# SSM output projection as three products of halves, normalisation on ScalarE, halves split on VectorE and GpSimd, x reloaded after the stage

## The reference, cut to what matters

```python
proj = x @ Wi                                  # 256 -> 512 (xs) + 64 (B) + 64 (C)
xc = silu(causal_conv(xs, cw, 4 taps) + cb)    # depthwise over the tokens
h = A * h + u_t * b_t ; y = h . c_t            # scan over 128 tokens, A = -0.5
x = layer_norm(y @ Wo + x) * g + b             # Wo: 512 -> 256
```

## Time and profile before

| | value |
|---|---|
| median of 3 runs | 1272.3 us (1270.44 to 1274.01) |
| profiled execution | 1271.9 us, span 1270.2 us |
| mean granted TensorE clock | 0.955 |
| TensorE busy, whole span | 1136.6 us (89%) |
| VectorE, ScalarE, GpSimd busy | 835.3 us (66%), 650.7 (51%), 663.3 (52%) |
| output projection L303 | 640 passes, 143.5 us |
| DMA | 53.73 MB, 42 GB/s on average |

### The profile page before, as it was taken

How to read it: one execution, slowest core, us unless ns; L and a number is a source line. 1 busy time by engine, 2 the same in 40 slices (tenths; PEclk the granted TensorE clock), 3 DMA queues, 4 the chain that set the end, 5 groups by cost and what they waited for, 6 DMA issues and landing times.

```text
span 1270.2 us, 21225 instructions
## 1 busy us (share of the span) xinstructions
PE 1136.6 (89%) x6835; PEld 886.8 (70%) x6835; DVE 835.3 (66%) x1882; ACT 650.7 (51%) x1905; POOL 663.3 (52%) x705
## 2 busy tenths in 40 slices
PE   3999999999996999999997699984699999986984
PEld 3788888888885788888876477763366666655862
DVE  6788988889883666666676578875433333324795
ACT  2555555555542655555555388882122444224873
POOL 3175766757653224334254577661357556642664
PEclk9999999999997999999999799996799999997995
DMA  4001001010100000000010123610523222322001
GB/s 149 20 1 58 23 17 62 17 62 0 34 2 0 1 2 1 1 1 1 1 51 18 59 76 126 250 43 33 143 43 49 44 43 43 50 34 67 1 26 42
DMA packets 38206, 53.73 MB, mean 42 GB/s; under 512 B 8448, under 2 KB 33024, under 8 KB 36576
## 3 DMA queue, kind: packets, MB, share of 16 engines
q1 hardware_dynamic: 29376, 42.28, 10.0%
q0 software_dynamic: 8736, 10.25, 5.1%
HBM read 40.78 MB, written 11.74 MB: 41 GB/s over the span
## 4 chain that ended last, share of the span: by engine, by line
PE 43%; ACT 7%; issue 7%; DVE 7%; POOL 3%; DMA 1%; POOLq 0%; ACTq 0%; DVEq 0%
PE bank L1515 11%; PE bank L1532 5%; ACT x_prob L1182 5%; PE bank L44 4%; PE bank L46 3%; PE bank L45 3%; PE bank L643 2%; PE bank L671 2%; PE bank L654 1%; PE bank L1272 1%; PE bank L1524 1%; PE bank L2001 1%; PE bank L1285 1%; POOL a_prob L810 1%; PE bank L1213 1%
## 5 line engine op out<-in xcount | busy, mean ns | idle before, releaser
L414 DVE SCALAR_TENSOR_TENSOR ssm_conv<-bank,conv_w,ssm_conv 128x508 f32<-128x508 f32 (+2 forms) x240 | 159.2, 729 | 10.1 <-ACT ssm_conv L350 10.1
L704 ACT ACTIVATE a_prob<-a_prob,a_neg_max 128x128 f32<-128x128 f32 x256 | 99.7, 391 | 117.8 <-DVE a_neg_max L750 117.8
L1515 PE MATMUL bank<-expert_raw,x_kept_next_t 128*128 x312 | 148.5, 599 | 1.2 <-ACT x_kept_next_t L1594 1.2
L303 PE MATMUL bank<-w_out,ssm_u 128*128 128x256 f32 x640 | 143.5, 382 | 0.0
L810 POOL TENSOR_TENSOR a_prob<-a_prob,a_inv 128x512 f32<-128x512 f32 x64 | 66.7, 1042 | 136.3 <-DVE a_inv L755 136.3
L303 PEld LDWEIGHTS bank<-w_out,ssm_u 128*128 128x128 f32 x640 | 119.9, 190 | 17.9
L508 POOL TENSOR_TENSOR act_t_lo<-ssm_turned,act_t_hi 128x512 fp32r<-128x512 f32 x40 | 51.6, 1290 | 97.5 <-ACT ssm_turned L375 97.5
L1459 POOL DMA_INDIRECT x_rows<-e_y,e_index x39 | 62.9, 1612 | 75.2 <-ACT e_y L1622 71.6
L1738 DVE COPY e_h_t<-bank 128x512 f32<-128x512 f32 x39 | 27.0, 692 | 105.3 <-PE bank L1524 102.0
L1182 ACT ACTIVATE x_prob<-bank,x_neg_max 128x128 f32<-128x128 f32 x256 | 89.9, 403 | 11.5 <-DVE x_neg_max L1159 11.5
L1069 POOL TENSOR_TENSOR x_prob<-x_prob,x_inv 128x512 f32<-128x512 f32 x64 | 67.1, 1054 | 42.1 <-DVE x_inv L1163 41.6
(11 more groups left out here) (328 smaller groups left out, 3010.2 us busy)
## 6 DMA issues: line engine op xcount, KB each, us to landing
expert_raw<-in_experts_laid SPq DMA_DIRECT2D x8, 1536.0 KB, 8.2
attn_raw<-in_attn_w_laid SPq DMA_DIRECT2D x4, 1024.0 KB, 7.6
w_in_raw<-in_L_attn_in_proj_w SPq DMA_DIRECT2D x5, 640.0 KB, 8.4
w_out<-in_L_attn_out_proj_w SPq DMA_DIRECT2D x5, 512.0 KB, 3.9
x_res<-in_x SPq DMA_DIRECT2D x4, 512.0 KB, 5.6
x_context<-in_ctx_t_laid SPq DMA_DIRECT2D x8, 256.0 KB, 3.8
z_rows<-x_kept_next_z SPq DMA_DIRECT2D x8, 256.0 KB, 2.1
x_rows<-x_res SPq DMA_DIRECT2D x8, 256.0 KB, 2.4
```

The costliest lines, as they stand in the source:

```text
L303: mm = pe.matmul(UWY[h][:, s * D:(s + 1) * D], u[:, g % 2, c, t:t + P], w_out[:, c, :], start=(c == 0), stop=(c == KI - 1))
L414: op = dve.scalar_tensor_tensor(out=acc, in0=xs, scalar=conv_w[:, c, TAPS - 1 - back:TAPS - back], in1=acc, op0=ALU.mult, op1=ALU.add)
L704: e = act.activation(prob[:, m % 4, i, :], prob[:, m % 4, i, :], ACT.Exp, bias=neg_max[:, m % 4, i:i + 1], accum_out=total[:, m % 4, i:i + 1])
L1515: mm = pe.matmul(bank[:, :], rows_t[:, t % 2, k, :], W[:, bass.ds(at + (column + k * FFN), FFN)], start=(k == 0), stop=(k == KD - 1))
```

## The change

- The output projection becomes `product`: w_out and u are each held as a high and a low half in fp32r. ScalarE writes silu(conv) twice, as `u_hi` and whole, in place, into `conv`; GpSimd subtracts (`split_u`) into `u_lo`. ScalarE makes w_out's high half, VectorE its low half, once a layer.
- The low half of the turned rows is taken by VectorE straight from the bank; `ssm_turned` and its copy go.
- The normalisation goes from VectorE to ScalarE, as res x rstd + shift with shift = -mean x rstd made by GpSimd for all four sequences of a group at once. It is done in the group after, between taps 1 and 2 of the next group. `finish` (ln_g, ln_b) moves with it.
- w_in is split in two parts, in group 2 of a layer.
- u_hi takes the memory of x, which is loaded again when the attention stage begins; GpSimd waits for it (`attn_ln_loaded` 48) before its attention work. `attn_raw` holds all four weights (4 MB, one transfer) in the memory of their low halves.
- GpSimd's loop over layers is written out. A constant of -1 is made at the start.

Names of semaphores, the declarations of tiles, and helpers that only move are left out of the diff.

```diff
-def split_w_in(pool, mem, layer, in_use=None):
+def split_w_in(pool, mem, layer, part, in_use=None):
...
+    chunks = lambda x: x[:, :, :].rearrange("p k (c n) -> p k c n", n=P)[:, :, (slice(0, KI + 1, KI), slice(1, KI))[part], :]
+    if part == 0:
+        pool.wait_ge(names["w_in_loaded"], layer * 16 + 16)
+        if in_use is not None:
+            pool.wait_ge(in_use, layer * GROUPS * KI)
+    pool.tensor_copy(chunks(hi), chunks(raw)).then_inc(names["w_in_split"], 1)
...
-                sp.wait_ge(names["w_in_split"], layer + 1)
+                sp.wait_ge(names["w_in_split"], layer * 4 + 4)
...
-                sp.wait_ge(uw_ready, layer * (2 * GROUPS) + 2 * GROUPS)
+                sp.wait_ge(names["w_out_split"], layer * 2 + 2)
                 mem["load_w_out"](sp, layer + 1)
-                sp.wait_ge(mem["attn_w_split"], layer * GROUPS + GROUPS)
...
+            sp.dma_start(mem["attn_raw"][:, :, :], io["attn_w_laid"].rearrange("a p n -> p a n")).then_inc(mem["attn_w_loaded"], 16)
             with sp.Fori(0, LAST) as layer:
-
-                sp.dma_start(mem["attn_raw"][:, :], io["attn_w_laid"][bass.ds(layer, 1)].rearrange(
-                    "a p n -> p (a n)")).then_inc(mem["attn_w_loaded"], 16)
...
-                pe.wait_ge(names["w_in_split"], layer + 1)
+                pe.wait_ge(names["w_in_split"], layer * 4 + 2)
...
                                  k == 0, k == KD - 1)
                 mm.then_inc(bc_ready, 1)
                 for c in range(KI):
+                    if c == 1 and g == 0:
+                        pe.wait_ge(names["w_in_split"], layer * 4 + 4)
...
-                    pe.wait_ge(tr_copied, n * 2 + h)
+                    pe.wait_ge(tr_low, n * 2 + h)
...
-                pe.wait_ge(u_ready, n * KI + KI)
+                pe.wait_ge(u_split, n * KI + KI)
                 if g == 0:
-                    pe.wait_ge(names["w_out_loaded"], layer * 16 + 16)
+                    pe.wait_ge(names["w_out_split"], layer * 2 + 2)
...
                         for c in range(KI):
-                            mm = pe.matmul(UWY[h][:, s * D:(s + 1) * D], u[:, g % 2, c, t:t + P],
-                                           w_out[:, c, :], start=(c == 0), stop=(c == KI - 1))
+                            mm = product(pe, UWY[h][:, s * D:(s + 1) * D], [x[:, g % 2, c, t:t + P] for x in (u_hi, u_lo)],
+                                         [x[:, c, :] for x in w_out], c == 0, c == KI - 1)
                     mm.then_inc(uw_ready, 1)
...
-                for c in range(KI):
+
+            def taps(layer, g, chunks, first=False):
+                n = layer * GROUPS + g
+                for c in chunks:
                     act.wait_ge(xs_ready, n * KI + c + 1)
                     if not (first and g == 0):
-                        act.wait_ge(u_ready, n * KI - KI + c + 1)
+                        act.wait_ge(u_split, n * KI - KI + c + 1)
...
-                    nc.scalar.activation(u[:, g % 2, c, :], conv[:, c, :], ACT.Silu).then_inc(u_ready, 1)
+                    act.activation(u_hi[:, g % 2, c, :], conv[:, c, :], ACT.Silu)
+                    act.activation(conv[:, c, :], conv[:, c, :], ACT.Silu).then_inc(u_ready, 1)
+
+            def split_w_out(layer):
+                act.wait_ge(names["w_out_loaded"], layer * 16 + 16)
+                act.activation(w_out[HI][:, :, :], mem["w_out_raw"][:, :, :], ACT.Copy).then_inc(names["w_out_split"], 1)
+
+            def normalise(layer, g):
+                n = layer * GROUPS + g
+                act.wait_ge(shift_ready, n + 1)
+                for h in range(2):
+                    for s in range(2):
+                        i = 2 * h + s
+                        act.activation(res[:, h, s, :], res[:, h, s, :], ACT.Identity, bias=shift[:, i:i + 1],
+                                       scale=rstd[:, i:i + 1]).then_inc(z_ready, 1)
...
-                act.activation(ACT_T[HI][:, :, t:t + 2 * P], bank, ACT.Copy)
-                if not (layer_is(layer, 0) and g == 0 and h == 0):
-                    act.wait_ge(tr_low, n * 2 + h)
-                act.activation(turned[:, :, :], bank, ACT.Copy).then_inc(tr_copied, 1)
-
+                act.activation(ACT_T[HI][:, :, t:t + 2 * P], bank, ACT.Copy).then_inc(tr_copied, 1)
+
+            split_w_out(0)
             front(0, 0, first=True)
+            taps(0, 0, range(KI), first=True)
             silu(0, 0, range(KI), first=True)
 
             def layer_steps(layer):
                 first, last = layer_is(layer, 0), layer_is(layer, LAST)
                 for g in range(GROUPS):
                     ahead = (layer, g + 1, first) if g < GROUPS - 1 else None if last else (layer + 1, 0)
+                    before = (layer, g - 1) if g > 0 else None if first else (layer - 1, GROUPS - 1)
                     if ahead:
                         front(*ahead)
+                        taps(*ahead[:2], range(0, 2), *ahead[2:])
+                    if before:
+                        normalise(*before)
                     if ahead:
+                        taps(*ahead[:2], range(2, KI), *ahead[2:])
                         silu(*ahead[:2], range(0, 2), *ahead[2:])
                     copy_uw(layer, g, 0)
                     copy_uw(layer, g, 1)
-                    before = (layer, g - 1) if g > 0 else None if first else (layer - 1, GROUPS - 1)
                     if before:
                         copy_turned(*before, 0)
+                    if g == GROUPS - 1 and not last:
+                        split_w_out(layer + 1)
                     if ahead:
                         silu(*ahead[:2], range(2, KI), *ahead[2:])
                     if before:
                         copy_turned(*before, 1)
             layers(act, layer_steps)
+            normalise(LAST, GROUPS - 1)
...
-                    dve.wait_ge(stats_ready, n * 4 + 2 * h + 2)
-                    dve.sem_inc(stats_seen, 1)
-                    for s in range(2):
-                        dve.bn_aggr(mv[:, 2 * h + s, :], stats[:, 2 * h + s, :]).then_inc(aggr_ready, 1)
-                    dve.wait_ge(aggr_ready, n * 4 + 2 * h + 2)
-                    dve.tensor_scalar(ve[:, 2 * h:2 * h + 2], mv[:, 2 * h:2 * h + 2, 1], EPS, None,
-                                      ALU.add).then_inc(var_ready, 1)
-                for h in range(2):
-                    dve.wait_ge(rstd_ready, n * 2 + h + 1)
-                    for s in range(2):
-                        i = 2 * h + s
-                        dve.tensor_scalar(res[:, h, s, :], res[:, h, s, :], mv[:, i, 0:1],
-                                          ve[:, i:i + 1], ALU.subtract, ALU.mult).then_inc(z_ready, 1)
+                if not (layer_is(layer, 0) and g == 0):
+                    dve.wait_ge(z_ready, n * 4)
+                dve.wait_ge(stats_ready, n * 5 + 4)
+                dve.sem_inc(stats_ready, 1)
+                for i in range(GS):
+                    dve.bn_aggr(mv[:, i, :], stats[:, i, :]).then_inc(aggr_ready, 1)
+                dve.wait_ge(aggr_ready, n * 4 + 4)
+                dve.tensor_scalar(rstd, mv[:, 0:GS, 1], EPS, None, ALU.add).then_inc(var_ready, 1)
+
+            def split_w_out(layer):
+                dve.wait_ge(names["w_out_split"], layer * 2 + 1)
+                dve.tensor_tensor(w_out[LO][:, :, :], mem["w_out_raw"][:, :, :], w_out[HI][:, :, :].bitcast(F32),
+                                  ALU.subtract).then_inc(names["w_out_split"], 1)
+
+            def turned_low(layer, g, h):
+                n = layer * GROUPS + g
+                t = g * GT + 2 * h * P
+                dve.wait_ge(tr_copied, n * 2 + h + 1)
+                dve.tensor_tensor(ACT_T[LO][:, :, t:t + 2 * P], TR[:, :].rearrange("p (k t) -> p k t", k=KD),
+                                  ACT_T[HI][:, :, t:t + 2 * P].bitcast(F32), ALU.subtract).then_inc(tr_low, 1)
+
...
                     decayed(layer, g)
                     if ahead:
                         convolve(*ahead, 1)
+                    before = (layer, g - 1) if g > 0 else None if first else (layer - 1, GROUPS - 1)
+                    if before:
+                        turned_low(*before, 0)
                     norm(layer, g)
+                    if before:
+                        turned_low(*before, 1)
+                    if g == GROUPS - 1 and not last:
+                        split_w_out(layer + 1)
             layers(dve, layer_steps)
+            for h in range(2):
+                turned_low(LAST, GROUPS - 1, h)
...
-            def finish(layer, g):
+            def invert(layer, g):
 
                 n = layer * GROUPS + g
-                for h in range(2):
-                    pool.wait_ge(var_ready, n * 2 + h + 1)
-                    pool.tensor_tensor(ve[:, 2 * h:2 * h + 2], ve[:, 2 * h:2 * h + 2], neghalf[:, 0:2],
-                                       ALU.pow).then_inc(rstd_ready, 1)
+                pool.wait_ge(var_ready, n + 1)
```

(82 more changed lines are left out.)

51 lines of the change are left out of this document (22 added, 29 removed).

## The result

The changed kernel takes 1249.4 us (1248.35 to 1250.04) beside 1271.8 of the kernel before (1270.44 to 1274.01): ratio 0.9825, interval 0.9811 to 0.9839, 22.4 us less. The forecast was 1254.5, range 1248 to 1267. The profiled execution took 1250.04, span 1248.2. A second measurement, with the last experiments, gave 1249.13 and 0.9823.

The account below looks back on a forecast made before the run. TensorE's queue was taken to bound the SSM stage. Gains of 18 x 1.14 = 20.5 and 0.25, less 1.0 for the end and 2.0 for lag, made 17.8 us: 1254.5 against the median, range 1248 to 1267.

Parts of the forecast that it names:

- own range: Whole kernel, if the main forecast holds without a rival: 1249.5 us with no cost, to 1260 with the larger costs.
- The bound and the product: SSM stage: TensorE's queue bounds; output projection takes 5.87 us for 7.01, saving 1.14 a group, to 16.46.
- Rival D: Output projection on TensorE: matmuls run at 109 ns, 0.53 us more gained in 20 groups, 1244 us; 3%.
- First group: Start of the SSM stage: doubled silus delay group 1's b by 1.1 us, so this group gains 0.25, not 1.14.
- The lag of GpSimd: Behind w_in's split, once a layer: late u and shift delay uw for TensorE, 0.5 us a layer, 2.0 in all.
- The end: End of the SSM stage: last u, norm, invert and ln passes run in sequence, costing 1.0 us more.
- Rival A: SSM groups: the loop of GpSimd and ScalarE becomes the bound, 7 to 14 us less gained, 1261 to 1268; 24%.
- Rival B: SSM groups: GpSimd's loop costs more than 17.60 us, so the kernel gets slower, 1279 us; 6%.
- Rival C: SSM groups: path not shortened; ScalarE's late copy delays b, low half delays turn 1; 1269 to 1276 us; 7%.
- it just fits: ScalarE's last turned copy ends 1.5 us into the next group; the next b is ready at 1.65.
- VectorE and w_out's low half: VectorE makes w_out's low half once a layer, bounds 1.4 and, waiting for a GpSimd pass, 2.7 us.
- x and attn_raw: Loads for attention: x under 14.5 us with cover 26, attn_raw 15 to 30 us; cost nothing, attn_raw 1 at worst.

Follow-up runs that it names:

- a1: The changed kernel with its output projection as 16 fp32 products again, on the high halves alone; 1273.6 us, ratio 1.0022.
- b1: The kernel before with its output projection as 48 single-pass matmuls on stand-in operands, no step moved to another engine; 1246.4 us, ratio 0.9809.
- p1: The changed kernel plus one unneeded 128x256 GpSimd subtraction in each group of layers 0 to 3; 1253.1 us, ratio 0.9861.
- p2: The changed kernel plus one unneeded 128x512 GpSimd subtraction in each group of layers 0 to 3; 1260.7 us, ratio 0.9915.
- a3: The changed kernel with the low halves of the turned rows subtracted on GpSimd again, with ScalarE's second copy; 1285.0 us, ratio 1.011.
- s2: The changed kernel plus two unneeded 128x1024 ScalarE copies per group, ahead of its last copy of turned rows; 1252.9 us, ratio 0.9855.

## Why the prediction was right, point by point

The measured 1249.4 lies within the stated range, but at the lower end of the "own range" of 1249.5 to 1260: the mechanism was right, and nearly every cost that was set against the gain was too high.

**The bound and the product.** Right. 5.79 us measured for 5.87, a group of 16.44 for 16.46; a1 and b1 show that this term alone makes the gain. 18 groups gave 19.53 + 1.21 = 20.7 where the sum had 20.5. The pitch is 0.118, with 0.11 more in the first step. Rival D took 109 ns. The Trainium skill's page "TensorE: Matmul & The Clock Gate", section "Back-to-back issue gap", has these 109 ns (262 cycles) for 256 columns as the gap of an isolated matmul, and says that in a stream of weight loads and matmuls both set the spacing. The 118 here, weight loads included, lie above the isolated gap, in line with the second; D used the first where it doesn't hold.

**First group.** Mis-sized: 1.41 saved (0.35 + 1.06), where the sum had 0.25. The step that failed is "the last two silus still begin at 41.8, which moves group 1's b by 1.1". ScalarE's timeline of the changed kernel:

```profile
41.05 0.63 ACT L365 ACTIVATE ssm_u_hi<-ssm_conv 128x512 fp32r<-128x512 f32 x1 [0.42 <-DVE ssm_conv L440]
...
43.15 0.58 ACT L345 ACTIVATE ssm_b_t<-bank 64x512 f32<-64x512 f32 x1
```

The taps are done 0.73 earlier, at 41.05, and b is copied at 43.15 where it was at 42.97, 0.18 later and not 1.1. The first product starts at 45.54, earlier than the 45.92 of the earlier trace rows, not at 46.5. Nor does the 0.25 follow from the forecast's own numbers: 46.5 for 45.92 would leave 1.14 - 0.58 = 0.56.

**The lag of GpSimd.** The mechanism was right, its price was 0 and not 2.0. The timelines of GpSimd and ScalarE behind a split of w_in, in the changed kernel:

```profile
224.60 0.19 POOL L517 TENSOR_TENSOR ve<-mv,neg_one 128x4 f32<-128x4 f32 x1
224.76 1.01 POOL L518 TENSOR_TENSOR ve<-ve,neghalf 128x4 f32<-128x4 f32 x1
...
226.08 2.08 ACT L378 ACTIVATE ssm_res<-ssm_res,ve 128x256 f32<-128x256 f32 x4 [2.89 <-POOL ve L520]
228.07 1.43 ACT L356 ACTIVATE ssm_conv<-bank,conv_b,conv_w 128x512 f32<-128x512 f32 x2
229.39 0.62 ACT L365 ACTIVATE ssm_u_hi<-ssm_conv 128x512 fp32r<-128x512 f32 x1
229.91 0.62 ACT L366 ACTIVATE ssm_conv<-ssm_conv 128x512 f32<-128x512 f32 x1
...
231.47 1.14 ACT L384 ACTIVATE ssm_uw<-bank 128x512 f32<-128x512 f32 x2
```

ScalarE waits 2.89 us for the shift, as foreseen. But u ends at 224.6, at 6.7 in the forecast's count, where it had 5.9 to 7.2, and from there to the first copied half of uw (232.04) it is 7.4 us, not 8.1. A silu costs 0.52 from start to start, not 0.58, and the invert 1.48, not 1.8 (a pow of four columns takes 1.01, where the earlier trace rows had 1.19). L317 starts at 232.25 as TensorE comes to it. By the forecast's prices the same u would have cost 6.7 + 8.1 - 14.4 = 0.4, near the 0.5 a layer that it took. The loop while GpSimd is behind, from invert to invert, is 224.60 to 239.41, 14.8 us for the 15.1 forecast.

**The end.** Forecast 1.0 lost, 0.27 measured. The mechanism was right (the last u is waited for, then norm, invert, norms, passes, turn one behind the other, as the gap of 7.67 us shows). Two terms were large: the norm is there 0.4 earlier, and the invert is some 0.25 shorter.

**Those four terms** are 0.2 + 1.2 + 2.0 + 0.7 = 4.1 us, which is the whole distance from the 17.8 of the sum to the 21.9 by which the profiled executions differ. All went one way, since the unknowns were taken dear.

**Rival A** didn't come true: a u half costs 1.25 from start to start, not 1.30 to 1.36. p1 and p2 put it 0.3 to 0.5 us a group away. **Rival B** didn't come true either; a3, with one more GpSimd operation per turned half, shows what it would look like, 1285. **Rival C** didn't come true: between the first group and the last none waits for b or for turn 1, and s2 disproves its half on ScalarE. Its failed step is "it just fits": it took the moment at which b is ready for the moment at which b is needed.

**VectorE and w_out's low half.** Right in size, 1.80 measured for bounds of 1.4 and 2.7. The timeline of VectorE in the changed kernel, first alone, then beside GpSimd:

```profile
28.14 1.22 DVE L476 TENSOR_TENSOR w_out_lo<-w_out_raw,w_out_hi 128x1024 fp32r<-128x1024 f32 x1 [1.39 <-ACT w_out_hi L370]
...
237.16 1.07 DVE L472 TENSOR_SCALAR ve<-mv 128x4 f32<-128x4 f32 x1
238.14 0.68 DVE L483 TENSOR_TENSOR act_t_lo<-bank,act_t_hi 128x512 fp32r<-128x512 f32 x1
238.74 1.80 DVE L476 TENSOR_TENSOR w_out_lo<-w_out_raw,w_out_hi 128x1024 fp32r<-128x1024 f32 x1
```

Alone it takes 1.22 and beside GpSimd's passes 1.80. By the Trainium skill's page "SBUF — State Buffer", section "SBUF: two separate sides", the two engines take a shared port pair in turns; the trace agrees. It also shows what the forecast left out: the small L472 takes 1.07 where it takes 0.17 with GpSimd idle (363.46), and GpSimd's four-column L517 beside L476 takes 1.19 at 239.41 where it takes 0.19 at 224.60. TensorE lost nothing by either.

**x and attn_raw.** Free, as forecast: x takes 8.7 us (under 14.5 forecast), and the 4 MB of attn_raw 12.4 (15 to 30 forecast).
